# The mask of the first scores in the third layer's attention: added in VectorE's fused maximum instead of by products on TensorE

## The chip, the cores and the metric

The kernel runs on one core of a Trainium2 chip. The metric is the device time of one execution in microseconds, the median of several executions; less is better. TensorE (PE in the profile) does matrix products out of SBUF into PSUM, PEld is its loading of weights, VectorE (DVE) and ScalarE (ACT) work on SBUF and PSUM, GpSimd (POOL) works on SBUF, and SyncE (SP) issues DMAs.

## The reference

The kernel computes a network of four layers; each layer adds an attention branch and a feed-forward branch to `x`. Only the attention of the third layer is touched:

```python
B, T, C = x.shape                      # 4, 1024, 128
nh, hd = (NUM_HEAD, C // NUM_HEAD)     # 16 heads of 8
q, k, v = ...                          # x @ Wq, x @ Wk, x @ Wv, split in heads
attn = jnp.einsum('bhqd,bhkd->bhqk', q, k) / jnp.sqrt(jnp.float32(hd))
bias = slopes[:, None] * (jnp.arange(T, dtype=jnp.float32) - (BLOCK_SIZE - 1))
attn = attn + bias[None, :, None, :]
causal = jnp.tril(jnp.ones((T, T), dtype=bool))
masked = jnp.where(causal[None, None], attn.astype(jnp.float32), jnp.finfo(jnp.float32).min)
probs = jax.nn.softmax(masked, axis=-1)
out = jnp.einsum('bhqk,bhkd->bhqd', probs, v)
```

The softmax needs the maximum of each query's row of masked scores.

## The kernel before, in words

Everything touched is in `alibi_attention` (line 792), one stage of the third layer. Queries, keys, the bias and, later, the row maximum are held as stacks of 54 bf16 rows for each head, so that one product over 54 rows gives fp32 scores. Two heads lie in rows 0 to 53 and 64 to 117 (`ROW`), and their two products run side by side in the array. The work goes in 16 items (`IT`) of 4 heads (`HU`), each of 1024 queries by 1024 keys, cut into blocks of 128 and chunks of 512 (`CH`; `CT` is 4 blocks).

Each item is computed in two passes. The **first scores** (`first`, line 924 on; its product is L937) have queries in the partitions: for each of 12 pairs of a query block and a key chunk (`sunits`, `STEPS` is 12) and each of the 4 heads a tile of 128 queries by up to 512 keys is written to one of three PSUM banks (`pS`, `SB` is 3; a_S in the trace), and VectorE reduces it to one maximum for each query (`maximum`, L1058). Eight of the 12 steps hold the diagonal block, as the last 128 of their 512, 384, 256 or 128 columns; for these, after the two products of a pair of heads, two more products (L943, the identity times `maskq`) add −3e38 above the diagonal, and only these release VectorE (`ring_in`). The order of steps is (3,0) (2,0) (1,0) (0,0) (4,0) (5,0) (6,0) (7,0) (7,1) (6,1) (5,1) (4,1), a query block and a key chunk each; the steps (4,0) to (7,0) have no diagonal. The maxima of the second chunk go to `mx2`, and one `tensor_tensor` (L1061) takes the larger of both chunks before TensorE transposes the maxima (`turn_maxima`, L950) and VectorE negates them (`rows`, L1069). GpSimd splits them into three bf16 parts (L881 to L887), and SyncE writes these into the stack by six DMAs (L908).

The **second scores** (`second`, L963, with their own mask products L967) have keys in the partitions; ScalarE takes their exponentials (`exponentials`, L1028), and TensorE weighs the values with these (`weigh`, L978, fp32). ScalarE copies the sums out (`empty`, L1034), TensorE transposes them (`turn_out`, L987), into a bank of the same ring of three, and VectorE divides (`normalise`, L1075 and L1077).

The order on every engine is written out by hand. First the lead: all 12 first steps of item 0 and the first 6 (`LEAD`) of item 1, with nothing between. Then for each item 12 steps n, each on TensorE: a second product pair, first products of heads 0 and 1, a second product pair, the weighing of the step before, first products of heads 2 and 3. At n = 6 to 11 the first products are those of steps 0 to 5 of the item after the next, at n = 0 to 5 those of steps 6 to 11 of the next item (`ahead`); so n = 10, 11, 0, 1 have the steps without the diagonal. `turn_out` comes at the end of n = 1 and n = 5, `turn_maxima` at the end of n = 6. The banks are taken in the order of `take`: a tile goes in only when the tile three places before it in that order has been read (`ring_out`).

The change touches: the constants built by GpSimd (L870 to L877), `first` (L937, L943), the wait in `turn_maxima`, and `maximum` (L1058, L1061). The prediction also uses the fused add and extremum that `attention` has for the second layer (L650): one `tensor_tensor_reduce` that reads scores in PSUM and an fp32 table in SBUF, writes the sum to SBUF and leaves the minimum; it shows as CUSTOM_DVE_ANT_0, and its result is delivered by a DVE_READ_ACCUMULATOR2_ANT behind it.

Of the kernel before, what the change touches and what calls it, by code (L numbers as in the profile page):

```python
# [6 lines left out]
BF16 = mybir.dt.bfloat16  # L7
U32 = mybir.dt.uint32
I32 = mybir.dt.int32
ALU = mybir.AluOpType  # L10
ACT = mybir.ActivationFunctionType
AX = mybir.AxisListType
# [779 lines left out]
def alibi_attention(nc, G, V9, qstack, kstack, w1, w2):  # L792
# [11 lines left out]
    mix = G["XR"][:, :, :].rearrange("p a b -> p (a b)").rearrange("p (i t c) -> p i t c", i=IT, t=TT)  # L804
    QS = [ph.sb(f"QS{s}", [P, HW, T], BF16) for s in range(NS)]
    KS = [ph.sb(f"KS{s}", [P, HW, T], BF16) for s in range(NS)]
    identb, maskq, maskk = (ph.sb(n, [P, P], BF16) for n in ("identb", "maskq", "maskk"))
    zeros = w2[:, 0:CH]
    NP = 4
    PT = w1[:, 0:NP * 2 * CH].rearrange("p (s v t) -> p s v t", s=NP, v=2)  # L810
# [19 lines left out]
    zeroed, consts, cleared = ph.sem("zeroed"), ph.sem("consts"), ph.sem("cleared")  # L830
    stack_in = [ph.sem(f"stackin{s}") for s in range(NS)]
    mrow_in = [ph.sem(f"mrowin{s}") for s in range(NS)]
    ring_in, ring_out, m_all, m_part, m_row = (ph.sem(n) for n in ("ringin", "ringout", "mall", "mpart", "mrow"))
    e_ps, e_sb, weighed, o_sb, r_inv = (ph.sem(n) for n in ("eps", "esb", "weighed", "osb", "rinvs"))

    def ahead(it, n):
# [30 lines left out]
    with nc.Block() as block:  # L867
        @block.gpsimd
        def _(pool):
            pool.memset(zeros, 0.0).then_inc(zeroed, 1)  # L870
            pool.tensor_copy(identb[:, :], G["ident"][:, :]).then_inc(consts, 1)
            pool.memset(maskq[:, :], 0.0).then_inc(consts, 1)
            pool.memset(maskk[:, :], 0.0).then_inc(consts, 1)
            pool.wait_ge(consts, 3)
            pool.affine_select(out=maskq[:, :], in_=maskq[:, :], compare_op=ALU.is_ge, fill=-3.0e38,
                               base=0, pattern=[[-1, P]], channel_multiplier=1).then_inc(consts, 1)
            pool.affine_select(out=maskk[:, :], in_=maskk[:, :], compare_op=ALU.is_ge, fill=-3.0e38,  # L877
                               base=0, pattern=[[1, P]], channel_multiplier=-1).then_inc(consts, 1)
            for it in range(IT):
                pool.wait_ge(ring_out, SB + ring["m", it] + 1)  # L880
                pool.tensor_copy(mrow[:, 0, :], minus).then_inc(m_part, 1)  # L881
                pool.wait_ge(m_part, it * 3 + 1)
                pool.tensor_tensor(res, minus, mrow[:, 0, :], ALU.subtract).then_inc(m_part, 1)
                pool.wait_ge(m_part, it * 3 + 2)
                pool.tensor_copy(mrow[:, 1, :], res).then_inc(m_part, 1)
                pool.wait_ge(m_part, it * 3 + 3)
                pool.tensor_tensor(mrow[:, 2, :], res, mrow[:, 1, :], ALU.subtract).then_inc(m_row, 1)  # L887
# [37 lines left out]
        def _(pe):  # L925
            def first(it, k, pair):

                i, c = sunits[k]
                s = it % NS
                if k == 0 and pair == 0:  # L930
                    pe.wait_ge(stack_in[s], (it // NS + 1) * LOADS)
                n = min((c + 1) * CH, (i + 1) * P) - c * CH
                diag = c == i // CT
                at = ring["s", it, k, 2 * pair]
                for half in range(2):
                    pe.wait_ge(ring_out, at + half + 1)
                    ins = pe.matmul(pS[(at + half) % SB][:, 0:n], QS[s][ROW[half], pair, i * P:(i + 1) * P],  # L937
                                    KS[s][ROW[half], pair, c * CH:c * CH + n], start=True, stop=not diag)
                    if not diag:
                        ins.then_inc(ring_in, 1)  # L940
                if diag:
                    for half in range(2):
                        pe.matmul(pS[(at + half) % SB][:, n - P:n], identb[:, :], maskq[:, :], start=False, stop=True)\  # L943
                          .then_inc(ring_in, 1)

            def turn_maxima(it):
                at = ring["m", it]
                pe.wait_ge(m_all, it + 1)
                pe.wait_ge(ring_out, at + 1)
                pe.transpose(pS[at % SB][0:ROWS, 0:P], mx[:, it % NS, :, :, :].rearrange("p h w t -> p (h w t)"),  # L950
                             G["ident"][:, :]).then_inc(ring_in, 1)

# [95 lines left out]
        @block.vector  # L1048
        def _(dve):
            def maximum(it, k):  # L1050
                i, c = sunits[k]
                s = it % NS
                n = min((c + 1) * CH, (i + 1) * P) - c * CH
                for u in range(HU):
                    at = ring["s", it, k, u]
                    peak = mx[:, s, u % 2, u // 2, i:i + 1] if c == 0 else mx2[:, s, u % 2, u // 2, i - CT:i - CT + 1]
                    dve.wait_ge(ring_in, at + 1)
                    dve.tensor_reduce(peak, pS[at % SB][:, 0:n], AX.X, ALU.max).then_inc(ring_out, 1)  # L1058
                if k == STEPS - 1:
                    dve.wait_ge(ring_out, SB + at + 1)  # L1060
                    dve.tensor_tensor(mx[:, s, :, :, CT:TT], mx[:, s, :, :, CT:TT], mx2[:, s, :, :, :], ALU.max)\  # L1061
                       .then_inc(m_all, 1)

            def rows(it):
                at = ring["m", it]
                dve.wait_ge(ring_in, at + 1)
                if it:
                    dve.wait_ge(m_row, it)
                dve.tensor_scalar(minus, pS[at % SB][0:ROWS, 0:P], -1.0, None, ALU.mult).then_inc(ring_out, 1)  # L1069

            def normalise(it, c):
                at = ring["o", it, c]
                v = pS[at % SB][:, :].rearrange("p (t u d) -> p t u d", t=CT, u=HU)
                dve.wait_ge(ring_in, at + 1)
                dve.reciprocal(rinv[:, c, :, :], v[:, :, :, 8]).then_inc(r_inv, 1)  # L1075
                dve.wait_ge(r_inv, 2 * it + c + 1)
                dve.tensor_tensor(mix[:, it, c * CT:(c + 1) * CT, :].rearrange("p t (u d) -> p t u d", u=HU), v[:, :, :, 0:8],  # L1077
                                  rinv[:, c, :, :].unsqueeze(3).to_broadcast([P, CT, HU, 8]), ALU.mult).then_inc(ring_out, 1)

            dve.sem_inc(ring_out, SB)  # L1080
            for k in range(STEPS):
                maximum(0, k)
            for k in range(LEAD):
                maximum(1, k)
                if k == 0:
                    rows(0)
            for it in range(IT):
                for n in range(STEPS):
                    if ahead(it, n):
                        maximum(*ahead(it, n))  # L1090
                    if n == 1 and it:
                        normalise(it - 1, 1)
                    if n == CT + 1:
                        normalise(it, 0)
                    if n == LEAD and it + 1 < IT:
                        rows(it + 1)
            normalise(IT - 1, 1)
# [1104 lines left out]
```

## Time and profile before

| | |
|---|---|
| median of 3 runs | 3312.41 us (3310.73 to 3314.17) |
| the profiled execution, its own time | 3321.7 us |
| its span | 3320.0 us |
| TensorE busy, share of the span | 2658.5 us, 80% |
| VectorE busy | 1770.7 us, 53% |
| ScalarE busy | 1332.9 us, 40% |
| GpSimd busy | 876.4 us, 26% |
| mean granted TensorE clock | 0.883 |

The profiled execution took 9.3 us more than the median; the rows of the trace are those of that execution. The stage of the change runs from 2104 to 2696 us of the span, 18% of it, so the shares of the whole say little about it: it is read by windows and in order of time. A line `[0.86 <-DVE a_mx L1058]` gives the idle time of an engine just before an instruction and what ended it. Idle time of PEld is mostly time in which TensorE is still streaming the product before. A granted clock of 1.00 is 2.4 GHz, 0.50 is 1.2 GHz.

### The profile page before, as it was taken

Reading aid. Unit: us, or ns where it says so; the run is one execution under the profiler, and the core shown is the slowest. Engines: PE = TensorE matmul, PEld = TensorE weight load, DVE = VectorE, ACT = ScalarE, POOL = GpSimd, SP = SyncE. Lnnn points to the kernel's source line nnn. Section 1 sums busy time; section 2 is a strip of 40 time slices with the busy share of each in tenths; the row PEclk is TensorE's granted clock in tenths of the full one; section 3 lists DMA queues with packets and bytes.
Section 4 is the critical chain, followed back from the end, with each engine's and each line's share of the span. In section 5 each row is a group of like instructions: output and inputs, shape, how many; then the busy total and the mean of one; then the engine's idle time right before and its main releaser. Section 6 shows DMA issues by size and latency. Waiting matters only on the chain. (4 is left out here: it accounts for less than half of the span.)

```text
span 3320.0 us, 49708 instructions
## 1 busy us (share of the span) xinstructions
PE 2658.5 (80%) x17202; PEld 1500.4 (45%) x17202; DVE 1770.7 (53%) x4428; ACT 1332.9 (40%) x2638; POOL 876.4 (26%) x1043
## 2 busy tenths in 40 slices
PE   4379998989999999999974572699999966656655
PEld 2246667976666666666651351233333332222222
DVE  5345553215555555555556013667777726685684
ACT  2135554435555555555551121155555542102102
POOL 0125554434555323232321303000000001241240
PEclk8579999989999999999985785589999978878777
DMA  2220002021011000000000105300101000000000
GB/s 107 49 94 27 29 27 74 27 93 33 27 15 26 1 14 1 15 1 1 1 3 9 32 8 99 110 23 23 34 23 27 19 27 0 0 0 0 0 0 25
DMA packets 75145, 93.56 MB, mean 28 GB/s; under 512 B 10002, under 2 KB 53140, under 8 KB 73252
## 3 DMA queue, kind: packets, MB, share of 16 engines
q1 hardware_dynamic: 65188, 77.94, 7.7%
q0 software_dynamic: 9728, 12.63, 2.2%
q8 instruction: 137, 2.24, 0.3%
q14 instruction: 92, 0.75, 0.1%
HBM read 54.60 MB, written 35.53 MB: 27 GB/s over the span
## 5 line engine op out<-in xcount | busy, mean ns | idle before, releaser
L1058 DVE TENSOR_REDUCE a_mx<-a_S 128x1 f32<-128x512 f32 (+3 forms) x768 | 385.0, 552 | 152.0 <-PE a_S L943 132.9
L1028 ACT ACTIVATE WA<-a_E 128x1024 f32<-128x1024 f32 (+3 forms) x384 | 303.3, 815 | 201.5 <-PE a_E L967 146.1
L490 PE MATMUL a1b_S<-a1b_Kf,a1b_Qf 64*128 64x512 f32 (+3 forms) x1160 | 306.9, 538 | 2.9 <-issue 2.9
L410 POOL TENSOR_SCALAR XR<-XR,a1b_rinv 128x384 f32<-128x384 f32 (+1 forms) x192 | 162.8, 865 | 343.1 <-DVE a1b_rinv L666 343.0
L592 ACT COPY a1b_PT<-a1b_T 128x512 f32<-128x512 f32 (+3 forms) x288 | 153.6, 533 | 236.6 <-PE a1b_T L500 234.1
L515 PE MATMUL a1b_O<-a1b_PT,WA 128*64 128x128 f32 x3456 | 231.1, 278 | 0.0
L937 PE MATMUL a_S<-a_KS,a_QS 54*128 54x512 bf16 (+3 forms) x768 | 195.1, 353 | 27.1 <-DVE a_mx L1058 15.6
L1852 PE MATMUL a_D<-a_Sr,WA 128*128 128x512 f32 x128 | 95.8, 891 | 135.3 <-POOL a_Sr L1836 135.3
L515 PEld LDWEIGHTS a1b_O<-a1b_PT,WA 128*64 128x64 f32 x3456 | 184.8, 136 | 29.9 <-issue 20.1
L410 POOL TENSOR_SCALAR WA<-WA,a1b_rinv 128x128 f32<-128x128 f32 (+1 forms) x194 | 124.1, 664 | 253.7 <-DVE a1b_rinv L666 253.5
L661 DVE COPY a1b_PT<-a1b_T 128x128 f32<-128x128 f32 (+3 forms) x288 | 140.6, 488 | 93.2 <-PE a1b_T L500 90.4
L500 PE MATMUL a1b_T<-ident,XR 128*128 128x128 f32 x1056 | 155.6, 280 | 31.7 <-ACT a1b_PT L592 31.4
L582 ACT ACTIVATE XR<-XR,a1b_nmax 128x384 f32<-128x384 f32 (+1 forms) x192 | 167.7, 875 | 26.4 <-DVE a1b_nmax L650 26.4
L650 DVE CUSTOM_DVE_ANT_0 XR<-a1b_S,a1b_tb 128x384 f32<-128x384 f32 (+1 forms) x192 | 118.6, 655 | 103.6 <-PE a1b_S L490 102.3
L978 PE MATMUL a_O<-WA,V 128*9 128x512 f32 (+3 forms) x1536 | 163.7, 499 | 0.0
L500 PEld LDWEIGHTS a1b_T<-ident,XR 128*128 128x128 f32 x1056 | 116.5, 141 | 90.2 <-issue 46.1
L582 ACT ACTIVATE WA<-WA,a1b_nmax 128x128 f32<-128x128 f32 (+1 forms) x196 | 128.6, 660 | 70.5 <-DVE a1b_nmax L650 64.2
L937 PEld LDWEIGHTS a_S<-a_KS,a_QS 54*128 54x128 bf16 x768 | 56.1, 94 | 217.7 <-DVE a_mx L1058 175.6
L490 PEld LDWEIGHTS a1b_S<-a1b_Kf,a1b_Qf 64*128 64x128 f32 x1160 | 121.7, 186 | 59.1 <-issue 48.2
L963 PE MATMUL a_E<-a_QS,a_KS 54*128 54x512 bf16 (+3 forms) x768 | 138.6, 337 | 8.4 <-ACT WA L1028 8.1
L881 POOL CAST a_mrow<-WA 32x128 bf16<-32x128 f32 x16 | 4.5, 281 | 527.8 <-DVE WA L1069 527.8
L666 DVE RECIPROCAL a1b_rinv<-a1b_rsum 128x2 f32<-128x2 f32 x193 | 32.1, 166 | 204.1 <-ACT XR L582 107.1
(417 smaller groups left out, 5220.9 us busy)
## 6 DMA issues: line engine op xcount, KB each, us to landing
WA<-in_w SPq DMA_DIRECT2D x8, 1024.0 KB, 9.8
a_QS<-qstack SPq DMA_DIRECT2D x32, 216.0 KB
a_KS<-kstack SPq DMA_DIRECT2D x32, 216.0 KB
a1b_tb<-tab SPq DMA_DIRECT2D x12, 512.0 KB
qstack<-a2s_parts SPq DMA_DIRECT2D x24, 256.0 KB
kstack<-a2s_parts SPq DMA_DIRECT2D x24, 256.0 KB
f_slots<-f1r_zrows SPq DMA_DIRECT2D x9, 516.0 KB
f1t_xs<-f_slots SPq DMA_DIRECT2D x9, 516.0 KB, 3.9
```

What stands on the lines that cost most here:

```text
L410: pool.tensor_scalar(soft(i0, u), soft(i0, u), rinv[:, n:n + 1], 1.0, ALU.mult, ALU.mult).then_inc(n_sb, 1)
L490: pe.matmul(pS[k % NB][:, 0:hi - lo], Qf[half, b0 % 2, i0 * P:(i0 + 1) * P], Kf[half, b0 % 2, lo:hi], start=True, stop=True).then_inc(s_ps, 1)
L500: ins = pe.transpose(pT[k % 2][:, j * P - lo:(j + 1) * P - lo], soft(i, u)[:, j * P:(j + 1) * P], G["ident"][:, :])
L515: ins = pe.matmul(pO[i // CT][half, i % CT * P:(i % CT + 1) * P], V[s][:, j, half], PT[:, i % 2 * HG + u, j * P:(j + 1) * P], start=(j == ...
L582: act.activation(soft(i0, u), soft(i0, u), ACT.Exp, bias=nmax[:, n:n + 1], scale=-1.0, accum_out=rsum[:, n:n + 1]).then_inc(p_sb, 1)
L592: act.copy(PT[:, i % 2 * HG + u, lo:hi], pT[0][:, 0:hi - lo]).then_inc(t_sb_a, 1)
L661: dve.tensor_copy(PT[:, i % 2 * HG + u, lo:hi], pT[1][:, 0:hi - lo]).then_inc(t_sb_d, 1)
L937: ins = pe.matmul(pS[(at + half) % SB][:, 0:n], QS[s][ROW[half], pair, i * P:(i + 1) * P], KS[s][ROW[half], pair, c * CH:c * CH + n], star ...
L963: ins = pe.matmul(pE[q % 2][:, half, off:CH], KS[s][ROW[half], q % 2, j * P:(j + 1) * P], QS[s][ROW[half], q % 2, c * CH + off:(c + 1) * C ...
L978: ins = pe.matmul(pO[32 * u:32 * u + 9, off:CH], V9[:, it, u, j, :], PT[:, (2 * n + u // 2) % NP, u % 2, off:CH], start=(j == 0), stop=(j ...
L1028: act.activation(PT[:, q % NP, :, off:CH], pE[q % 2][:, :, off:CH], ACT.Exp).then_inc(e_sb, 1)
L1058: dve.tensor_reduce(peak, pS[at % SB][:, 0:n], AX.X, ALU.max).then_inc(ring_out, 1)
```

## The change

The mask products of the first scores go. GpSimd builds `maskq` in fp32, 128 by 512: zeros, with the triangle in its last 128 columns. On the eight diagonal steps VectorE uses `tensor_tensor_reduce`: it adds the last n columns of `maskq` to the scores, writes the sum to one of two scratch tiles (`masked`), and leaves the maximum; on the second chunk the maximum starts from that of the first chunk, so the `tensor_tensor` over the maxima and its semaphore go too. Before each of these it waits for its own instruction two places earlier, which used the same scratch tile. The four steps without a diagonal keep `tensor_reduce`. The order of all steps stays.

```diff
-    identb, maskq, maskk = (ph.sb(n, [P, P], BF16) for n in ("identb", "maskq", "maskk"))
+    identb, maskk = (ph.sb(n, [P, P], BF16) for n in ("identb", "maskk"))
+    maskq, masked = ph.sb("maskq", [P, CH]), ph.sb("masked", [P, 2, CH])
...
-            pool.affine_select(out=maskq[:, :], in_=maskq[:, :], compare_op=ALU.is_ge, fill=-3.0e38,
+            pool.affine_select(out=maskq[:, CH - P:CH], in_=maskq[:, CH - P:CH], compare_op=ALU.is_ge, fill=-3.0e38,
...
                 for half in range(2):
                     pe.wait_ge(ring_out, at + half + 1)
                     ins = pe.matmul(pS[(at + half) % SB][:, 0:n], QS[s][ROW[half], pair, i * P:(i + 1) * P],
-                                    KS[s][ROW[half], pair, c * CH:c * CH + n], start=True, stop=not diag)
-                    if not diag:
-                        ins.then_inc(ring_in, 1)
-                if diag:
-                    for half in range(2):
-                        pe.matmul(pS[(at + half) % SB][:, n - P:n], identb[:, :], maskq[:, :], start=False, stop=True)\
-                          .then_inc(ring_in, 1)
+                                    KS[s][ROW[half], pair, c * CH:c * CH + n], start=True, stop=True)
+                    ins.then_inc(ring_in, 1)
 
             def turn_maxima(it):
                 at = ring["m", it]
-                pe.wait_ge(m_all, it + 1)
-                pe.wait_ge(ring_out, at + 1)
+                pe.wait_ge(ring_out, max(at, SB + ring["s", it, STEPS - 1, HU - 1]) + 1)
...
-                    peak = mx[:, s, u % 2, u // 2, i:i + 1] if c == 0 else mx2[:, s, u % 2, u // 2, i - CT:i - CT + 1]
+                    peak = mx[:, s, u % 2, u // 2, i:i + 1]
+                    before = mx2[:, s, u % 2, u // 2, i - CT:i - CT + 1]
                     dve.wait_ge(ring_in, at + 1)
-                    dve.tensor_reduce(peak, pS[at % SB][:, 0:n], AX.X, ALU.max).then_inc(ring_out, 1)
-                if k == STEPS - 1:
-                    dve.wait_ge(ring_out, SB + at + 1)
-                    dve.tensor_tensor(mx[:, s, :, :, CT:TT], mx[:, s, :, :, CT:TT], mx2[:, s, :, :, :], ALU.max)\
-                       .then_inc(m_all, 1)
+                    if c < i // CT:
+                        dve.tensor_reduce(before, pS[at % SB][:, 0:n], AX.X, ALU.max).then_inc(ring_out, 1)
+                    else:
+                        if at >= 2:
+                            dve.wait_ge(ring_out, SB + at - 1)
+                        dve.tensor_tensor_reduce(out=masked[:, at % 2, 0:n], in0=pS[at % SB][:, 0:n], in1=maskq[:, CH - n:CH], scale=1.0,
+                                                 scalar=before if c else -3.0e38, op0=ALU.add, op1=ALU.max,
+                                                 accum_out=peak).then_inc(ring_out, 1)
...
             dve.sem_inc(ring_out, SB)
+            dve.wait_ge(consts, 5)
```

## Rows read from the trace of the kernel before

**Rows 1.** Busy time by windows: PE, PEld, DVE, ACT, POOL, clock, DMA, GB/s.

```profile
2112.00:2156.00 44.00, 39.71 (x122) 10.63 (x123) 34.70 (x72) 0.00 (x0) 1.39 (x4) 0.50 0.11 37
2152.00:2156.00 4.00, 3.76 (x10) 0.91 (x10) 3.83 (x8) 0.00 (x0) 0.00 (x0) 0.50 0.00 0
2156.00:2180.00 24.00, 23.47 (x125) 6.03 (x123) 13.96 (x28) 11.20 (x14) 0.00 (x0) 0.50 0.00 0
2184.20:2218.20 34.00, 32.39 (x266) 10.96 (x265) 25.34 (x54) 19.97 (x26) 1.40 (x4) 1.00 0.10 28
```

**Rows 2.** GpSimd in order of time: first cast of each item.

```profile
2184.22 0.28 POOL L881 CAST a_mrow<-WA 32x128 bf16<-32x128 f32 x1 [36.83 <-DVE WA L1069]
...
2626.65 0.28 POOL L881 CAST a_mrow<-WA 32x128 bf16<-32x128 f32 x1 [32.41 <-DVE WA L1069]
```

**Rows 3.** Groups of instructions by form, 2112 to 2662 us.

```profile
L937 PEld LDWEIGHTS a_S<-a_KS,a_QS 54*128 54x128 bf16 x768 | 56.1, 94 | 217.7 <-DVE a_mx L1058 175.6 <-issue 28.9
```

**Rows 4.** In order of time: start, duration; one diagonal hand-off, n = 2 into 3.

```profile
2307.34 0.10 PEld L937 LDWEIGHTS a_S<-a_KS,a_QS 54*128 54x128 bf16 x2 [0.65 <-DVE a_mx L1058]
...
2307.66 0.11 PEld L943 LDWEIGHTS a_S<-a_maskq,a_identb 128*128 128x128 bf16 x2 [0.23 <-issue]
...
2307.88 0.10 PEld L963 LDWEIGHTS a_E<-a_QS,a_KS 54*128 54x128 bf16 x2
...
2307.94 2.30 DVE L1058 TENSOR_REDUCE a_mx<-a_S 128x1 f32<-128x512 f32 x4 [0.45 <-PE a_S L943]
...
2308.68 0.09 PEld L937 LDWEIGHTS a_S<-a_KS,a_QS 54*128 54x128 bf16 x1 [0.33 <-DVE a_mx L1058]
```

**Rows 5.** In order of time: steps without the diagonal.

```profile
2295.04 8.68 DVE L1058 TENSOR_REDUCE a_mx<-a_S 128x1 f32<-128x512 f32 x14 [0.32 <-PE a_S L937]
...
2303.84 0.39 PE L937 MATMUL a_S<-a_KS,a_QS 54*128 54x512 bf16 x2
...
2304.27 1.29 DVE L1058 TENSOR_REDUCE a_mx<-a_S 128x1 f32<-128x512 f32 x2 [0.55 <-PE a_S L937]
```

**Rows 6.** In order of time: the fused minimum of the second layer's attention.

```profile
1300.71 0.08 DVE L650 DVE_READ_ACCUMULATOR2_ANT a1b_nmax<- 128x1 f32 x1
1300.71 0.75 DVE L650 CUSTOM_DVE_ANT_0 XR<-a1b_S,a1b_tb,a1b_firstmax 128x512 f32<-128x512 f32 x1
1301.39 0.08 DVE L650 DVE_READ_ACCUMULATOR2_ANT a1b_nmax<- 128x1 f32 x1
...
1314.35 0.92 PE L490 MATMUL a1b_S<-a1b_Kf,a1b_Qf 64*128 64x384 f32 x4
...
1315.45 0.56 DVE L650 CUSTOM_DVE_ANT_0 XR<-a1b_S,a1b_tb 128x384 f32<-128x384 f32 x1 [4.43 <-PE a1b_S L490]
...
1318.21 0.69 DVE L650 CUSTOM_DVE_ANT_0 XR<-a1b_S,a1b_tb 128x512 f32<-128x512 f32 x1
...
1318.83 0.08 DVE L650 DVE_READ_ACCUMULATOR2_ANT a1b_nmax<- 128x1 f32 x1
```

**Rows 7.** Weight loads in order of time: second scores at n = 5.

```profile
2314.03 0.10 PEld L963 LDWEIGHTS a_E<-a_QS,a_KS 54*128 54x128 bf16 x2 [0.47 <-ACT WA L1028]
```

**Rows 8.** Order of time: second scores of n = 0 and n = 6, item 0, then item 4.

```profile
2155.87 0.13 PEld L963 LDWEIGHTS a_E<-a_QS,a_KS 54*128 54x128 bf16 x2
...
2180.03 0.10 PEld L963 LDWEIGHTS a_E<-a_QS,a_KS 54*128 54x128 bf16 x2 [0.18 <-issue]
...
2298.46 0.12 PEld L963 LDWEIGHTS a_E<-a_QS,a_KS 54*128 54x128 bf16 x2
...
2316.16 0.10 PEld L963 LDWEIGHTS a_E<-a_QS,a_KS 54*128 54x128 bf16 x2 [0.17 <-issue]
```

**Rows 9.** Busy time by windows, as in rows 1: where the stage runs out.

```profile
2675.10:2678.50 3.40, 1.81 (x24) 0.43 (x16) 0.00 (x0) 2.91 (x5) 0.00 (x0) 0.95 0.00 0
2678.50:2682.00 3.50, 3.50 (x18) 0.96 (x16) 0.22 (x1) 1.58 (x2) 0.00 (x0) 0.56 0.02 5
```

**Rows 10.** SyncE in order of time: the six DMAs of item 0's maxima.

```profile
2146.07 3.77 SPq L908 DMA_DIRECT2D a_QS<-a_mrow  x6
```

More of the change, by code:

```diff
@@ L832, in alibi_attention @@
     mrow_in = [ph.sem(f"mrowin{s}") for s in range(NS)]
-    ring_in, ring_out, m_all, m_part, m_row = (ph.sem(n) for n in ("ringin", "ringout", "mall", "mpart", "mrow"))
+    ring_in, ring_out, m_part, m_row = (ph.sem(n) for n in ("ringin", "ringout", "mpart", "mrow"))
     e_ps, e_sb, weighed, o_sb, r_inv = (ph.sem(n) for n in ("eps", "esb", "weighed", "osb", "rinvs"))
@@ L932, in first @@
                 n = min((c + 1) * CH, (i + 1) * P) - c * CH
-                diag = c == i // CT
                 at = ring["s", it, k, 2 * pair]
```

## The prediction

> **What bounds the kernel now.** The change lies in one stage, so I read it first by windows [rows 1]. In a steady item TensorE is busy 32.39 of 34.00 us, VectorE 25.34, ScalarE 19.97: TensorE comes first, but its busy time contains the tails of products, and the waits show that it isn't alone. The items repeat exactly: the first cast of an item on GpSimd comes 13 periods apart between 2184.22 and 2626.65, 34.03 us each [rows 2]. The groups by form tell what TensorE waits for: its weight loads for the first scores are ended by VectorE's reads for 175.6 us in sum [rows 3]. So two things set the period, TensorE's own queue and the ring of three banks. One hand-off in order of time shows how they mesh [rows 4]: heads 2 and 3 of a diagonal step start at 2307.34, their masks at 2307.66, the next product at 2307.88; VectorE starts at 2307.94, 0.60 after the products, and the bank that its first read frees lets head 1 of the next step start at 2308.68, 1.34 after. What TensorE has to do in those 1.34 us decides whether it waits. On the four steps without a diagonal VectorE is the bound: 14 reads in 8.68 us without a gap, less than 0.62 each [rows 5].
>
> So an item has two parts. From n = 10 to n = 1 (9.2 us, from the first halves without a mask to the last ones at 2303.84) VectorE's rate sets the time. From there to the next n = 10 (24.8 us) lie the eight diagonal steps, and TensorE or the hand-off sets it.
>
> **What is removed.** A mask pair holds TensorE for 0.22 us (2307.66 to 2307.88 [rows 4]); an item has 16, so at most 3.5 us. Since both heads are released only by it, VectorE also starts later: 0.60 us after the products with masks, 0.43 without (2303.84 to 2304.27) [rows 4, 5]. The `tensor_tensor` over the maxima and its wait lie beside other work, except in the lead (0.2 us, estimate).
>
> **What is added.** VectorE's own rate hardly changes. The second layer's fused instruction on 512 columns has its accumulator read 0.62 us after its start, and the next fused instruction starts together with that read (both at 1300.71); started from a column of another tile it is 0.68 (1300.71 to 1301.39) [rows 6]. So the fused form costs 0.01 more in the first chunk, 0.07 in the second, some 1.3 us over an item, for a VectorE that idles over 8 us. The bank comes free at the end of the read: 0.70 and 0.76 after the start, against 0.69 for the reduction.
>
> What costs is the start. A plain reduction starts 0.04 us after the last product ends (2303.84 + 0.39, then 2304.27 [rows 5]). The fused one starts 0.18 after it (1314.35 + 0.92, then 1315.45 [rows 6]), 0.14 more, whenever VectorE was idle, and here it is behind two waits. The second wait, for its own instruction two places before, is met long before (at 0.76 of 1.24 us), but it has to be passed; bound it between 0 and another 0.14, I take 0.04. Hand-off in the second chunk: 1.34 − 0.17 + 0.18 + 0.07 = 1.42 us, so it gets no shorter; in the first chunk 1.36.
>
> On this cost a rule of the Trainium skill speaks otherwise: VectorE: DVE Perf Modes, section "The DRAIN you can't avoid", says that a semaphore after each copy costs nothing extra. By that the start would cost nothing and the period would fall by 2.5 us instead of 1.5. Rows 6 show 0.18 against 0.04 and I go by them.
>
> **The walk through the eight diagonal steps.** From the last unmasked products at 2303.84, time on TensorE until each step's products of heads 2 and 3: a mask of heads 0 and 1 always comes out (0.22), a mask of heads 2 and 3 only where the next step doesn't then wait for its bank.
> - n = 2, 3, 4: the mask of heads 0 and 1 comes out of each, less 0.05 for the longer hand-off; the mask of heads 2 and 3 shortens only the wait for the bank. 0.5 us.
> - n = 5: the second scores wait for ScalarE until 2314.03 [rows 7], and ScalarE follows the weighing of the step before, so it keeps the 0.5 and adds nothing; the mask ahead of the transposes adds 0.22, total 0.7.
> - n = 6 to 9: each pair of masks leaves 0.43 us, the next wait for a bank takes back half: 0.2 each, total 1.5 at n = 10.
>
> Taken from the other end, 7 of the 16 pairs come through. Lower bound 0.9 (each wait costs 0.28 more instead of 0.18), upper 2.5 (no start cost), and 3.5 if nothing waited. The part without a diagonal stays. Period 32.5 us.
>
> **The rest of the stage.** Lead: VectorE is busy 34.70 of 44.00 us in it [rows 1], idle 9.3, of which 1.1 before the first read. It becomes VectorE-bound, as the unmasked steps show, since three banks give the start cost time. 8.2 back, minus 16 reads of the second chunk at 0.07, plus about 1 for tails counted as busy: 8. Behind it the second scores need the maxima's DMAs: issued from 2146.07 on [rows 10], no traffic in 2152 to 2156 [rows 1], so landed 6 us after; the second scores start 9.8 after [rows 8], and only 2 of the lead's 8 come out between. Covered, by 1.8. GpSimd's larger `maskq` has 5 us of cover before the first product. Item 0 up to n = 5 runs at 1.2 GHz with TensorE full (23.47 of 24.00 [rows 1]): 8 pairs at some 0.33, estimate between 0.22 and 0.44, 2.6; its second half 0.8. Item 14 has half the steps, 0.7.
>
> Sum: 8 + 2.6 + 0.8 + 13 × 1.5 + 0.7 = 31.6. The profiled execution of 3321.7 would become 3290; from the median of 3312.4, 9.3 lower, it is **3281 us**, 1.0% faster. I use the difference, since other stages stay.
>
> **Rivals.**
> - *No start cost, or more slack than I see* (period falls 2.5 to 3.5): 8.7 + 3.4 + 33 to 45 + 1 gives 3254 to 3266. For it: the skill's rule; against it: rows 6.
> - *The hand-off eats the loop's gain* (0.3 a period): what stays is the lead and item 0, 12 + 4: 3296. It needs a start cost near 0.3.
> - *The fused instruction's preparation is not hidden* behind the one before, so VectorE pays 0.14 or more on each of its 512, or up to 0.28: 32 × 0.14 = 4.5 us an item beside 25.34 busy of 34 [rows 1], which fills most of its idle time; the gain of the loop is gone and the lead loses 48 × 0.14 = 6.7 of its 8. About 3310, no change. Against: in rows 6 the next one starts with the read of the one before.
> - *The clock, slower than before.* Item 0's second scores of n = 0 to n = 6 took 24.16 us at 1.2 GHz, 17.70 in item 4 at 2.4 GHz [rows 8], 6.5 us more. TensorE stayed at 1.2 GHz from 2156 to 2180 although full [rows 1], and lost 2.4 GHz once late in the stage after a stretch in which it was busy 1.81 of 3.40 us [rows 9]. Without the masks it has less to do around n = 3 to 5. If it falls there once in each period and stays down for half an item, that is 13 × 6.5 = 84: 3365. It decides from five such halves on (31.6 / 6.5); six and more are slower than before. Against: the steady item would still be busy about 29 of 32.5 us, far above the row that lost it. The Trainium skill, TensorE: Matmul & The Clock Gate, section "A second HAM failure mode: psum-queue depth-cycling", describes this case, TensorE idling briefly between groups while it cycles through banks and its clock going to and fro; the steady rows here show 1.00.
>
> **How the numbers follow.** Forecast (3268 to 3292) 0.62; no start cost (3254 to 3268) 0.13; only the lead (3292 to 3303) 0.10; preparation not hidden (about 3310) 0.06; the clock 0.09. Bounds of the forecast: 0.9 a period gives 3289, 2.4 gives 3269. The range 3263 to 3303 leaves out the far part of the first rival (0.04) and the last two (0.15). A measurement of this kernel tells 0.2% (6.6 us) from no change. Faster 0.84, within 0.2% 0.06, slower 0.10.
>
> **What would show it.** In the changed profile: no L943; casts of L881 32.5 us apart instead of 34.03; the fused instruction 0.62 and 0.68 apart when fed, and starting 0.18 to 0.22 after the products' end when not; wait of the weight loads for VectorE about as long as before, not shorter; the lead some 8 us shorter and without gaps on VectorE; the clock 1.00 from item 0's middle on. Wrong it would be if casts are under 31.6 or over 33.2 us apart, if fused instructions stand over 0.7 apart when fed, or if 0.50 appears inside the loop.

## The result, and the profile after

| | before | after |
|---|---|---|
| median | 3311.57 us (3309.31 to 3314.17) | 3267.77 us (3259.67 to 3273.24) |
| the profiled execution, its own time | 3321.7 us | 3270.57 us |
| its span | 3320.0 us | 3268.8 us |
| TensorE busy | 2658.5 us, 80% | 2592.1 us, 79% |
| VectorE busy | 1770.7 us, 53% | 1775.8 us, 54% |
| mean granted TensorE clock | 0.883 | 0.885 |

The ratio of the times is 0.9862, with an interval of 0.984 to 0.9884: the changed kernel is 1.4% faster, 43.8 us between the medians. The forecast was 3281 us, a gain of 31.6; the time lies in the range of 3263 to 3303.

In the changed kernel the reduction without a mask is L1054, the fused maximum L1058, the product of the first scores still L937, that of the second scores L957 and its mask L961, the weighing L972, the first cast of an item on GpSimd L882.

The loop first: GpSimd's casts in order of time, which answer to [rows 2]. From the cast at 2170.13 on the items are 30.98 or 30.99 us long, 3.05 less than 34.03; the one from 2325.05 to 2357.57 is an exception.

```profile
2140.43 0.28 POOL L882 CAST a_mrow<-WA 32x128 bf16<-32x128 f32 x1 [33.18 <-DVE WA L1067]
...
2170.13 0.28 POOL L882 CAST a_mrow<-WA 32x128 bf16<-32x128 f32 x1 [28.09 <-DVE WA L1067]
...
2201.11 0.28 POOL L882 CAST a_mrow<-WA 32x128 bf16<-32x128 f32 x1 [29.37 <-DVE WA L1067]
...
2325.05 0.28 POOL L882 CAST a_mrow<-WA 32x128 bf16<-32x128 f32 x1 [29.38 <-DVE WA L1067]
...
2357.57 0.28 POOL L882 CAST a_mrow<-WA 32x128 bf16<-32x128 f32 x1 [30.89 <-DVE WA L1067]
...
2574.45 0.28 POOL L882 CAST a_mrow<-WA 32x128 bf16<-32x128 f32 x1 [29.37 <-DVE WA L1067]
...
2605.43 0.28 POOL L882 CAST a_mrow<-WA 32x128 bf16<-32x128 f32 x1 [29.36 <-DVE WA L1067]
```

Next the windows, with the columns of [rows 1]: the lead, the 4 us in which item 0 has its clock back, a steady item, and the stretch before and in the exception of the list above.

```profile
2112.00:2148.00 36.00, 31.64 (x73) 7.13 (x73) 34.01 (x119) 0.00 (x0) 1.39 (x4) 0.50 0.14 45
2156.00:2160.00 4.00, 3.67 (x32) 1.07 (x28) 3.79 (x9) 1.59 (x3) 0.00 (x0) 0.95 0.00 0
2160.00:2180.00 20.00, 18.34 (x151) 5.29 (x151) 15.40 (x66) 13.86 (x17) 1.39 (x4) 1.00 0.01 2
2201.11:2232.10 30.99, 28.80 (x236) 8.70 (x233) 25.73 (x86) 19.84 (x27) 1.39 (x5) 1.00 0.11 31
2347.50:2350.95 3.45, 2.52 (x24) 0.83 (x27) 2.94 (x16) 3.09 (x4) 0.00 (x0) 1.00 0.00 0
2350.95:2354.36 3.41, 3.41 (x20) 1.11 (x12) 1.18 (x6) 1.42 (x3) 0.00 (x0) 0.50 0.00 0
```

VectorE fills the lead: 34.01 of 36.00 us busy, and 1.3 of the rest lie before its first read at 2113.26. TensorE has its full clock from 2156 on; before, it was at 0.50 until 2180 [rows 1].

Last, the fused instruction, in order of time. First a hand-off in the second chunk, n = 2 into 3, as in [rows 4]; then the wait for ScalarE at n = 5, behind which VectorE is idle; then two instructions of the first chunk that follow one another.

```profile
2189.34 0.10 PEld L937 LDWEIGHTS a_S<-a_KS,a_QS 54*128 54x128 bf16 x2 [0.64 <-DVE a_mx L1058]
2189.35 0.39 PE L937 MATMUL a_S<-a_KS,a_QS 54*128 54x512 bf16 x2
...
2189.77 0.75 DVE L1058 CUSTOM_DVE_ANT_0 a_masked<-a_S,a_maskq,a_mx 128x512 f32<-128x512 f32 x1
...
2190.59 0.33 PE L937 MATMUL a_S<-a_KS,a_QS 54*128 54x384 bf16 x1 [0.31 <-DVE a_mx L1058]
2190.59 0.39 PE L957 MATMUL a_E<-a_QS,a_KS 54*128 54x128 bf16 x2
2190.91 0.28 PE L961 MATMUL a_E<-a_maskk,a_identb 128*128 128x128 bf16 x2
...
2195.34 0.39 PE L957 MATMUL a_E<-a_QS,a_KS 54*128 54x512 bf16 x2 [0.49 <-ACT WA L1022]
...
2196.64 0.23 PE L937 MATMUL a_S<-a_KS,a_QS 54*128 54x128 bf16 x2
...
2196.91 0.35 DVE L1058 CUSTOM_DVE_ANT_0 a_masked<-a_S,a_maskq,a_mx 128x128 f32<-128x128 f32 x1 [1.39 <-PE a_S L937]
...
2198.03 0.69 DVE L1058 CUSTOM_DVE_ANT_0 a_masked<-a_S,a_maskq 128x512 f32<-128x512 f32 x1
...
2198.64 0.69 DVE L1058 CUSTOM_DVE_ANT_0 a_masked<-a_S,a_maskq 128x512 f32<-128x512 f32 x1
```

At 2196.64 + 0.23 the products end, at 2196.91 the fused instruction starts: 0.04 us, as a plain reduction. The products of 2189.35 are followed 0.42 later by their reader, as in [rows 5]. Fed, the instructions stand 0.61 apart. From the products of heads 2 and 3 at 2189.34 to the late product at 2190.59 (head 1 of the next step, which waits for its bank) it is 1.25 us; [rows 4] had 1.34.

### The profile page after: what moved, and what is told of

It is laid out like the page before. It is cut to its first block and busy times, and to the rows that moved or that the text cites. A ratio compares the mean times of both kernels' runs of the same rounds, so it can differ in the third digit from the quotient of the medians.

```text
span 3268.8 us, 49675 instructions
## 1 busy us (share of the span) xinstructions
PE 2592.1 (79%) x16690; PEld 1459.7 (45%) x16690; DVE 1775.8 (54%) x4924; ACT 1330.4 (41%) x2638; POOL 874.4 (27%) x1043
## 5 line engine op out<-in xcount | busy, mean ns | idle before, releaser
L937 PE MATMUL a_S<-a_KS,a_QS 54*128 54x512 bf16 (+3 forms) x768 | 204.0, 351 | 33.0 <-DVE a_mx L1058 20.0
L1054 DVE TENSOR_REDUCE a_mx<-a_S 128x1 f32<-128x512 f32 x256 | 157.4, 681 | 16.4 <-PE a_S L937 14.4
L937 PEld LDWEIGHTS a_S<-a_KS,a_QS 54*128 54x128 bf16 x768 | 60.5, 93 | 235.9 <-DVE a_mx L1058 130.9
L972 PE MATMUL a_O<-WA,V 128*9 128x512 f32 (+3 forms) x1536 | 163.5, 498 | 0.0
L957 PE MATMUL a_E<-a_QS,a_KS 54*128 54x512 bf16 (+3 forms) x768 | 153.9, 333 | 11.2 <-ACT WA L1022 10.9
L1058 DVE CUSTOM_DVE_ANT_0 a_masked<-a_S,a_maskq 128x512 f32<-128x512 f32 (+3 forms) x256 | 112.7, 488 | 52.6 <-PE a_S L937 52.4
```

The source lines that it names most:

```text
L957: ins = pe.matmul(pE[q % 2][:, half, off:CH], KS[s][ROW[half], q % 2, j * P:(j + 1) * P], QS[s][ROW[half], q % 2, c * CH + off:(c + 1) * C ...
L972: ins = pe.matmul(pO[32 * u:32 * u + 9, off:CH], V9[:, it, u, j, :], PT[:, (2 * n + u // 2) % NP, u % 2, off:CH], start=(j == 0), stop=(j ...
L1054: dve.tensor_reduce(before, pS[at % SB][:, 0:n], AX.X, ALU.max).then_inc(ring_out, 1)
```

## The experiments

Items are the distance between first casts of steady items; where some are longer, it is said beside. Each ratio is to the kernel before as it ran beside that kernel. The first four variants, the next four and the last two ran in three groups, in which the median of before was 3312.2, 3312.4 and 3316.8 us. The traces are one execution of each kernel.

| kernel | median, us | ratio to before | items, us |
|---|---|---|---|
| the change, once more | 3271.56 | 0.9867 (0.9835 to 0.99) | 30.98, two of 32.5 |
| an increment between the waits | 3293.21 | 0.9939 (0.9919 to 0.9959) | 31.89, six near 33.3 |
| idle products for all masks | 3314.95 | 1.0005 (0.9992 to 1.0018) | 33.79, two near 35.3 |
| halves of the second scores swapped | 3268.23 | 0.9858 (0.9821 to 0.9895) | 30.98, one of 32.5 |
| fused in the first chunk alone | 3287.89 | 0.9932 (0.9915 to 0.9948) | 32.09 |
| fused in the second chunk alone | 3310.82 | 0.9991 (0.9977 to 1.0006) | 32.7, from the third on 34.15 |
| idle products for heads 0 and 1 | 3316.47 | 1.0015 (1.0004 to 1.0025) | 33.33, five of 34.8, one of 36.0 |
| idle products for heads 2 and 3 | 3271.10 | 0.9885 (0.9868 to 0.9901) | 31.45 |
| second chunk alone, filled | 3291.10 | 0.9921 (0.9904 to 0.9938) | 32.79 |
| the change, filled | 3269.46 | 0.9857 (0.9836 to 0.9878) | 31.10, two of 32.6 |

**The change once more.** The changed kernel itself, run beside the next three.

> The changed kernel once more, beside the others. The items of the changed kernel's trace stood 30.98 us apart, against 34.03 before; the clock rose to 2.4 GHz at 2156 us, against 2180. Theory (the gain is made in the loop): items again 30.98 apart, wherever the clock rises. Rival (the earlier clock made a large part): if the clock rises later in this execution, the time moves by a large part of the 44 us; by the theory it moves by at most 5.

Measured: 3271.56 us, ratio 0.9867; items of 30.98 again, but now two of 32.52. The period is a property of the kernel, the longer items aren't: their number differs from one execution to the next. The clock came back at 2156 here too, so the rival, that the earlier clock made a large part of the gain, wasn't put to the test.

**Is there a start cost?** In the second layer an increment of a semaphore stands between the wait for the products and the fused instruction. This kernel puts one there.

```diff
                     if c < i // CT:
...
                     else:
                         if at >= 2:
                             dve.wait_ge(ring_out, SB + at - 1)
+                    if c == i // CT:
+                        dve.sem_inc(passed, 1)
```

> The changed kernel with a semaphore increment between the wait for the scores and each fused instruction, as the second layer's loop has it. Theory: the start cost of 0.14 us that I read from that loop belongs to the increment, which makes the wait an instruction of its own; here the fused instruction starts 0.18 instead of 0.04 after the products' end when VectorE was idle, and the items stand 31.4 to 32.0 us apart. Rival (the fused instruction itself has or hasn't the start cost whatever stands before it): start and items as in the changed kernel, 0.04 and 30.98.

Measured: items of 31.89 us, 0.91 more, ratio 0.9939. The 0.18 us of [rows 6] appear at the same place, in order of time: products from 2193.06 for 0.23, the fused instruction at 2193.47.

```profile
2193.06 0.23 PE L937 MATMUL a_S<-a_KS,a_QS 54*128 54x128 bf16 x2
...
2193.47 0.35 DVE L1060 CUSTOM_DVE_ANT_0 a_masked<-a_S,a_maskq,a_mx 128x128 f32<-128x128 f32 x1 [1.51 <-PE a_S L937]
```

So the 0.14 us that I read off the second layer belong to that increment, not to the fused instruction. The second wait of the changed kernel, which is met long before, adds nothing: the start is 0.04 with both. And my price of it was about right: I had put the difference between start cost and none at 1.0 us an item (2.5 against 1.5), and it is 0.91.

**Is it TensorE's queue or the earlier release?** The changed kernel, with two products of the mask's form in the queue ahead of the second scores that follow a diagonal pair. They write where the second scores write afterwards, and VectorE doesn't wait for them.

```diff
             def second(it, q):
...
+                behind = ahead(it, (q - 1) // 2) if q else None
+                if behind and sunits[behind[1]][1] == sunits[behind[1]][0] // CT:
+                    for half in range(2):
+                        pe.matmul(pE[q % 2][:, half, 0:P], identb[:, :], maskk[:, :], start=True, stop=True)
```

> The changed kernel with idle product pairs of the mask products' size put back on TensorE in the loop, just behind the place of the old ones, but into the bank of the second scores, so that they don't hold VectorE up (the lead has none). Theory (what the change gives back is TensorE's queue time): items 33.5 to 34.0 us apart, nearly all of the 3.05 lost again. Rival (the gain is VectorE's earlier release, 0.17 a hand-off): items 31 to 32 us apart.

Measured: items of 33.79 us, 2.81 of the 3.05 are gone. The other 0.24 is what is left for VectorE's release without the mask. So nearly all of the loop's gain is time in TensorE's queue. The idle pairs don't stand quite where the masks stood: they come behind the second scores' wait for ScalarE, the masks came ahead of it, and no run tells what that is worth.

The whole time, 3315 us, is that of before, and this isn't explained by the items. The lead has no idle products, and in the trace the stage takes 566.5 us from its first product (2107.56) to its last mask (2674.08), where before took 579.7 (2112.28 to 2691.97). What follows the stage took 637.7 us instead of 628.0. Other traces fall on either side too (637.7 in the repeat of the change, 629.0 in its first trace), and why isn't settled. So the items are the measure of these variants, and the whole time is a rough one.

**Which half of the masks?** The same products only behind heads 0 and 1, and only behind heads 2 and 3 of each diagonal step, eight an item in each.

```diff
-                behind = ahead(it, (q - 1) // 2) if q else None
+                behind = ahead(it, q // 2) if q % 2 else None
...
-                behind = ahead(it, (q - 1) // 2) if q else None
+                behind = ahead(it, q // 2 - 1) if q and q % 2 == 0 else None
```

> The changed kernel, plus two idle products of the mask's form in TensorE's queue only where the mask of heads 0 and 1 stood (8 an item; with all 16 items were 33.79 apart against 30.98). My walk in the prediction, freed of its start cost: a mask of heads 0 and 1 always counts in full (8 x 0.22 = 1.8), one of heads 2 and 3 only half or not: items 32.7 apart, ratio about 0.994. Rival 'no wait for a bank takes anything back': both kinds cost the same, 1.4: items 32.4, ratio about 0.993.

> The changed kernel, plus two idle products of the mask's form only where the mask of heads 2 and 3 stood (8 an item). My walk freed of its start cost: 0.5 to 0.8 (31.5 to 31.8 apart, ratio about 0.990). Rival 'no wait for a bank takes anything back': 1.4, items 32.4 apart, ratio about 0.993.

Measured: 33.33 and 31.45, so 2.35 and 0.47 us more than 30.98; together 2.82, what all sixteen cost. The walk had the mechanism right: a product behind heads 0 and 1 counts in full, one behind heads 2 and 3 is nearly absorbed by the wait for the bank (0.06 a pair). It had the price of the first kind wrong: 2.35 / 8 = 0.29 a pair, not 0.22. The whole time with the products behind heads 0 and 1 misses the expected ratio of 0.994; dearer pairs, six items with a fall of the clock (below) and 638.1 us behind the stage make it long. In order of time, the kernel with idle products behind heads 0 and 1, at the late product of n = 3:

```profile
2187.35 0.33 PE L937 MATMUL a_S<-a_KS,a_QS 54*128 54x384 bf16 x1 [0.31 <-DVE a_mx L1062]
2187.62 0.29 PE L957 MATMUL a_E<-a_maskk,a_identb 128*128 128x128 bf16 x2
2187.84 0.23 PE L961 MATMUL a_E<-a_QS,a_KS 54*128 54x128 bf16 x2
2188.00 0.29 PE L965 MATMUL a_E<-a_maskk,a_identb 128*128 128x128 bf16 x2
```

From the late product to the mask of the second scores it is 0.65 us here and 0.32 in the changed kernel (2190.59 to 2190.91 above), where the first product of the second scores starts together with the late one. Of the 0.33 between them the idle pair holds the queue for 0.22 (2187.62 to 2187.84); the other 0.11 is what the second scores gain by starting with the late product. The masks of before did the same as the idle pair: from the late product of [rows 4], at 2308.68, it was 0.65 us too.

```profile
2308.95 0.28 PE L943 MATMUL a_S<-a_maskq,a_identb 128*128 128x128 bf16 x2
2309.17 0.23 PE L963 MATMUL a_E<-a_QS,a_KS 54*128 54x128 bf16 x2
2309.33 0.28 PE L967 MATMUL a_E<-a_maskk,a_identb 128*128 128x128 bf16 x2
```

**Does that depend on which rows run side by side?** The late product takes one half of the array's rows, and so does each product of the second scores. I took it that the second scores can join only from the other half, and that their order would then matter.

```diff
-                for half in range(2):
+                for half in (1, 0):
                     ins = pe.matmul(pE[q % 2][:, half, off:CH], KS[s][ROW[half], q % 2, j * P:(j + 1) * P],
```

> The changed kernel with the two products of each second-score pair in the other order, rows 64 to 117 first. In the changed trace the single late product of a first-score pair (rows 64 to 117) starts together with the first product of the second scores (rows 0 to 53). Theory (this running side by side is the part of the gain beyond the mask's own 0.22 a pair): with the order turned they meet in the same rows and the items are 0.5 to 1.5 us longer, 31.5 to 32.5. Rival: order is nothing, items 30.98.

Measured: items of 30.98 and one of 32.5, as in the changed kernel: nothing moved. In order of time, at the same place:

```profile
2193.20 0.33 PE L937 MATMUL a_S<-a_KS,a_QS 54*128 54x384 bf16 x1 [0.31 <-DVE a_mx L1058]
2193.20 0.38 PE L957 MATMUL a_E<-a_QS,a_KS 54*128 54x128 bf16 x2
2193.52 0.28 PE L961 MATMUL a_E<-a_maskk,a_identb 128*128 128x128 bf16 x2
```

The order is nothing, but this doesn't refute the reading by rows. In either order one of the two products lies in the late one's rows and one in the others, and in both traces one starts with the late product and the second 0.17 behind it (the two together last 0.39 and 0.38 us, one alone some 0.22). What the traces do show is a difference between whole and half: the masks of before and the idle pairs, which take all 128 rows, start 0.27 us after a late product of 384 columns (2308.68 to 2308.95, 2187.35 to 2187.62), the second scores, which take 54, at once (2190.59, 2193.20). That fits the reading; no run isolates it.

**Each chunk alone.** The kernel before, with the fused maximum on the diagonal steps of one chunk and the products of the mask on those of the other; the second started from a constant, with the `tensor_tensor` over the maxima kept.

```diff
-                diag = c == i // CT
+                diag = c == i // CT and c != 0
...
-                    dve.tensor_reduce(peak, pS[at % SB][:, 0:n], AX.X, ALU.max).then_inc(ring_out, 1)
+                    if c == i // CT and c == 0:
...
+                        dve.tensor_tensor_reduce(out=masked[:, at % 2, 0:n], in0=pS[at % SB][:, 0:n], in1=maskf[:, CH - n:CH], scale=1.0,
+                                                 scalar=-3.0e38, op0=ALU.add, op1=ALU.max,
+                                                 accum_out=peak).then_inc(ring_out, 1)
```

(and with c = 1 in place of 0)

> The kernel before, with the fused maximum only on the four diagonal steps of the first chunk (c = 0, n = 6 to 9) and the products of the mask kept on those of the second. In the two traces n = 2 to 5 gave back 1.0 us an item and n = 6 to 10 gave 2.1. Theory 'each pair's queue time comes out where it stood': items 34.03 - 2.1 = 31.9 us apart, lead about half of its 8 us, sum about 31 us of the 44: ratio 0.991 (0.9895 to 0.9925). Rival 'a gain in one chunk shows only because the other chunk lost its masks too (slack handed on)': 0.8 to 1.5 an item, 32.5 to 33.2 apart, ratio 0.9935 to 0.996.

> The kernel before, with the fused maximum only on the four diagonal steps of the second chunk (c = 1, n = 2 to 5, started from a constant, the tensor_tensor over the maxima kept) and the products of the mask kept on those of the first. Theory 'each pair's queue time comes out where it stood': items 34.03 - 1.0 = 33.0 us apart, ratio about 0.9955 (0.994 to 0.997). Rival 'slack handed on': the first chunk alone or this one gives something else than 2.1 and 1.0; if this one gives 0 to 0.5 and the first chunk over 2.5, then the second scores' wait for ScalarE at n = 5 takes back what is saved before it. The two kernels together with the whole change test it: if the parts add up (near 3.05) nothing is handed on.

Measured: the first chunk gives 1.94 an item (32.09) for the 2.1 that the steps of the traces had said, and a ratio of 0.9932, just outside the 0.9895 to 0.9925. The second gives 1.3 in its first two items (32.80 and 32.67), 0.3 more than expected, and with 1.94 that makes 3.2, near 3.05: the parts add up. But from the third item on they are 34.15 long, longer than before the change, and the kernel is no faster. Its windows show why, with the columns of [rows 1], twice the stretch before and after that point of an item:

```profile
2266.43:2269.84 3.41, 2.32 (x23) 0.77 (x22) 2.92 (x18) 2.92 (x4) 0.00 (x0) 1.00 0.00 0
2269.84:2273.25 3.41, 3.41 (x18) 1.07 (x18) 0.90 (x6) 1.45 (x2) 0.00 (x0) 0.50 0.00 0
...
2300.56:2303.97 3.41, 2.33 (x24) 0.77 (x20) 3.04 (x18) 2.87 (x4) 0.00 (x0) 1.00 0.00 0
2303.97:2307.38 3.41, 3.41 (x18) 1.08 (x18) 0.85 (x6) 1.50 (x2) 0.00 (x0) 0.50 0.01 2
```

The granted clock falls to 1.2 GHz for 3.41 us, each time 26.6 to 26.8 us after the item's first cast, twelve items in a row, and costs 34.15 − 32.67 = 1.48 us each. This is the rival with the clock, at under a quarter of its price (6.5 us): it fell in each item, behind n = 3 to 5 as I had feared, but stayed down for 3.4 us and not for half an item. The longer items of the changed kernel are the same thing: 32.51 − 30.98 = 1.53, at 2350.95 in the windows above.

**What does the clock fall behind?** In order of time, the second chunk alone: the products before the fall wait for ScalarE.

```profile
2269.51 0.10 PEld L967 LDWEIGHTS a_E<-a_QS,a_KS 54*128 54x128 bf16 x2 [0.81 <-ACT WA L1032]
2269.51 0.39 PE L967 MATMUL a_E<-a_QS,a_KS 54*128 54x512 bf16 x2 [0.67 <-ACT WA L1032]
```

This is the wait of [rows 7], longer now that the masks ahead of it are gone. If idling there brings the clock down, products that do nothing should keep it up at no cost. Both kernels have the two idle products behind heads 2 and 3 of the four diagonal steps of the second chunk:

```diff
+                behind = ahead(it, q // 2 - 1) if q and q % 2 == 0 else None
+                if behind and sunits[behind[1]][1] == sunits[behind[1]][0] // CT == 1:
+                    for half in range(2):
+                        pe.matmul(pE[q % 2][:, half, 0:P], identb[:, :], maskk[:, :], start=True, stop=True)
```

> The kernel before with the fused maximum on the diagonal steps of the second chunk, plus two idle products of the mask's form after heads 2 and 3 of those four steps, where TensorE otherwise waits (0.67 us for ScalarE in the trace of the kernel without them; its clock is at 1.2 GHz for 3.4 us behind that wait in every item from the fourth on, and items are 34.15 apart instead of 32.67). Theory 'the clock falls because TensorE idles there': no fall inside an item, items 32.7 to 33.0 apart, ratio 0.9935 to 0.997 instead of 0.999. Rival 'the fall has to do with the item's length, not with that idling': items still about 34.1 apart, ratio about 0.999.

> The changed kernel, plus the same two idle products after heads 2 and 3 of the four diagonal steps of the second chunk. Theory 'the clock falls because TensorE idles there': no item of 32.5 us is left, items 31.0 to 31.3 apart (with the products after all eight steps they were 31.45), ratio 0.986 to 0.989, so no faster than the changed kernel, since one to three falls of 1.5 us are all there is to win. Rival: items of 32.5 us remain.

Measured: the second chunk alone is 0.7% faster with more to do, 3291.1 against 3310.8 us, and better than the expected ratio: no fall is left in its loop, and its items are 32.79. Not all of it is the loop. Of the 19.6 us between the two traces 16.3 lie between the casts of items 1 and 15, 4.8 before them, where the clock came back at 2158 instead of 2174, and behind them it is 1.4 slower. In the changed kernel items are 31.10, 0.12 dearer, and two falls remain, so the time is the same. One window ahead of a point like that, of the kernel that was cured, and one ahead of a fall that remained in the changed one:

```profile
2261.70:2265.10 3.40, 2.72 (x28) 0.98 (x26) 3.00 (x18) 2.78 (x4) 0.00 (x0) 1.00 0.00 0
```

```profile
2406.46:2409.87 3.41, 2.82 (x26) 0.99 (x24) 3.41 (x17) 2.59 (x4) 0.00 (x0) 1.00 0.01 2
2409.87:2413.28 3.41, 3.40 (x16) 1.16 (x17) 0.80 (x6) 1.78 (x2) 0.00 (x0) 0.50 0.00 0
```

TensorE's busy time doesn't sort them: 2.72 of 3.40 us without a fall, 2.82 of 3.41 with one. That the idling at n = 3 to 5 brings the clock down in the second chunk alone is shown, by its cure; what decides on the one or two falls of the changed kernel stays open. Idle products don't help wherever they stand: behind heads 0 and 1 there were six falls in the loop, behind heads 2 and 3 of all eight diagonal steps none, behind both two.

## Why the prediction was right, and its gain too small

The direction, the bound and the range held, but the prediction's picture of the loop did not. By its own signs it was wrong: the casts stand 30.98 us apart, under the 31.6 that it named, and 0.50 appears inside the loop, at 2350.95. The time of 3267.77 lies 0.2 inside the stretch that it gave to the rival without a start cost (3254 to 3268, chance 0.13), not in the forecast's own. And the 13 us between forecast and median owe something to luck: the two profiled executions, which the sum was made for, differ by 51.2 us instead of 31.6.

By parts, between the same instructions of the two profiled executions:

| part | forecast | measured |
|---|---|---|
| lead and item 0, to the cast of item 1 | 8 + 2.6 + 0.8 = 11.4 | 2184.22 − 2170.13 = 14.1 |
| 13 items | 13 × 1.5 = 19.5 | 442.43 − 404.32 = 38.1 |
| rest of the stage, to its last product | 0.7 | 65.1 − 65.2 = −0.1 |
| behind the stage | 0 | −0.9 |
| sum | 31.6 | 51.2 |

442.43 and 404.32 are 2184.22 to 2626.65 [rows 2] and 2170.13 to 2574.45; the last products of the second scores end at 2691.75 and 2639.62. The 38.1 are 13 × 3.05 less 1.5 for the one longer item. In the rest of the stage the last full item gave 1.05 (casts at 2626.65 and 2658.68 before, 2574.45 and 2605.43 after), and falls of the clock in the stretch behind it (mean 0.90 from 2605.40 to 2639.60) took it back. The 51.2 are 3320.0 − 3268.8; the profiled execution of before lay about 10 above its median and that of after 3 above its own, which leaves the 44 between the medians.

**What bounds the kernel**: right. TensorE's queue and the hand-off set the period together; the kernels with idle products show both, 0.29 a pair where the queue counts and 0.06 where the bank does.

**Lead**: right. The first product of the second scores starts at 2148.07 instead of 2155.90 (its weight load: 2155.87 [rows 8]), 7.8 less, and VectorE has no gap over 0.3 us. The maxima's DMAs, now issued from 2140.73 instead of 2146.07 [rows 10], stayed covered.

**Item 0**: forecast 3.4 with its second half, measured 14.1 − 7.8 = 6.3. The step missed the clock: it came back at 2156 instead of 2180, and I had let item 0 run at 1.2 GHz up to n = 5 as before. Half an item is 6.5 us shorter at 2.4 GHz [rows 8], so that alone covers the 2.9 that were missing. Why the clock came back earlier no run tells. In ten of the eleven traces with a fused maximum it came back between 2151 and 2160, in the second chunk alone at 2174, and of before there is one trace: it may be the change, or that one execution.

**The fused instruction's rate**: right. 0.61 and 0.67 apart when fed, for 0.62 and 0.68; the preparation is hidden.

**The start cost**: the step that failed. "The fused one starts 0.18 after it, 0.14 more" read a row rightly and gave the time to the wrong cause. In the second layer an increment stands between wait and instruction; here none does, and the start is 0.04. This took 1.0 from the forecast's gain an item, of the 1.55 by which it was short. The rule of the Trainium skill that I weighed against it (VectorE: DVE Perf Modes, section "The DRAIN you can't avoid": a semaphore after each copy costs nothing extra) would have given 2.5 us an item. The runs agree with it for an increment that is part of the instruction, as here, with its start of 0.04; one that stands by itself ahead of the fused ones costs 0.91 us an item.

**The walk**: right in its rule, short in one size. Without the start cost it gives 2.5, and 3.05 came out; a pair behind heads 0 and 1 is worth 0.29 instead of 0.22, and 8 × 0.07 is the difference. By the steps, in order of time, first of before, then of after:

```profile
2315.34 0.23 PE L937 MATMUL a_S<-a_KS,a_QS 54*128 54x128 bf16 x2
...
2328.65 0.39 PE L937 MATMUL a_S<-a_KS,a_QS 54*128 54x512 bf16 x2
```

```profile
2186.17 0.39 PE L937 MATMUL a_S<-a_KS,a_QS 54*128 54x512 bf16 x2
...
2207.79 0.52 PE L937 MATMUL a_S<-a_KS,a_QS 54*128 54x512 bf16 x2
```

From the last unmasked products to those of heads 2 and 3 at n = 5 it is 2315.34 − 2303.84 [rows 5] = 11.50 before and 2196.64 − 2186.17 = 10.47 after: 1.0, where I had 0.7. To the first ones at n = 10 it is 24.81 and 21.62: 3.2 in all, so 2.2 from n = 6 on, where I had 0.8. The part without a diagonal takes back 0.1. "7 of the 16 pairs come through" should have been 14: mask pairs behind heads 2 and 3 are absorbed (0.06 each), but those behind heads 0 and 1 are worth more than they hold the queue, and the hand-off became shorter, not longer.

**The wait of the weight loads**: I expected it to be about as long as before. It is 130.9 + 60.9 = 191.8 us for 175.6 [rows 3], so longer while the kernel is faster, as befits a queue with less in it. From the groups of after, 2112 to 2606 us:

```profile
L937 PEld LDWEIGHTS a_S<-a_KS,a_QS 54*128 54x128 bf16 x768 | 60.5, 93 | 235.9 <-DVE a_mx L1058 130.9 <-DVE a_mx L1054 60.9 <-issue 25.6
```

**The rivals.** *No start cost* was the right one for the loop: its 3254 to 3266 ends 1.8 under the median, and its 2.5 to 3.5 an item hold the 3.05. It would have deserved more than 0.13. *The hand-off eats the gain* and *preparation not hidden* fell. *The clock* was overrated in price: it takes 1.5 us from an item or two here, though it cost a partial version of this change all of its gain. The section of the Trainium skill that I named for it (TensorE: Matmul & The Clock Gate, "A second HAM failure mode: psum-queue depth-cycling") tells of a clock that goes to and fro because TensorE idles briefly. The second chunk alone agrees in that, with twelve falls; but the idle time ahead of them was a wait for ScalarE (0.67 us), not for a bank.

## What to carry to other kernels

Before a start-up cost is taken from another place in the code, look at what stands between the wait and the instruction there: an increment cost 0.14 us here, a second wait that had long been met nothing. Work taken out of an in-order queue counts in full behind the last thing that the queue waits for, and nearly nothing ahead of it; two kernels with idle work in the one place and in the other say which is which. And an engine with less to do can lose its clock: look at the granted clock behind the wait that has grown, and if it falls there in each round, try giving the engine something idle to do at that wait. In the changed kernel, which had few falls, it gained nothing.

## What the runs showed of the hardware

- A wait followed by an increment delays the fused VectorE instruction by 0.14 us when it is starved (0.18 against 0.04 from the products' end); 0.91 us over an item's 32 such instructions, most of which are fed.
- The accumulator read of a fused instruction (82 ns, 512 times) starts together with the next fused instruction where that one is fed (both at 2198.64), so it costs the rate nothing: 0.61 us from start to start on 512 columns from a constant, 0.67 from a column of another tile.
- A fall of the granted clock from 1.00 to 0.50 for 3.41 us costs 1.48 to 1.53 us, and it came at the same place of twelve items in a row. The same kernel with eight more small products an item keeps 1.00 in all of them and is 20 us faster, some 16 of them in the loop.
- Behind a late product over 54 rows and 384 columns, products over all 128 rows start 0.27 us later, products over 54 rows at once.
- TensorE's clock came up at 2156 in item 0 after the change and at 2180 before, one trace of before; the cause is open.
